# Routing with a scan on VectorE and the rank summed on TensorE, scatters and experts two steps earlier, in a bidirectional Mamba layer with a top-1 mixture of experts

## The chip, the cores and the metric

One core of one Trainium2 chip runs the whole program. The metric is the device time of one execution in microseconds (us). The five engines are TensorE (PE, with its weight loads PEld), VectorE (DVE), ScalarE (ACT), GpSimd (POOL) and SyncE (SP), which here issues nearly all plain DMAs. Each engine works through its own list of instructions in order and waits on semaphores.

## The reference

The input is x, 8 batches of 512 tokens with 128 features, all in float32. It is normalized once to xn, and the output is `x + attn(xn) + ffn(xn)`.

```
xn  = layernorm(x)
attn: xn2 = layernorm(xn)*g + b
      out_f = mamba(xn2), out_b = mamba(xn2 reversed in time), reversed back
      attn  = concat(out_f, out_b) @ combine_w.T + combine_b + xn
mamba: projection, causal convolution of 4 taps, silu, x_proj, softplus(dt), then per step t
      h = h * exp(delta_t * A) + (delta_t * u_t) * B_t ;  y_t = sum_n h[:, n] * C_t[n]
      y = (y + u * D) * silu(z) ;  y @ out_w.T
ffn:  e(token) = argmax over 8 experts of xn @ router_w.T      (the first of equals)
      ffn = down_w[e] @ ( silu(gate_w[e] @ xn) * (up_w[e] @ xn) )
```

The inner width of the Mamba is 256 and its state has 16 entries per channel. There are 4096 tokens in all.

## The kernel before

**The Mamba part sets the pace.** There are 16 units: each of the 8 batches forward and backward (`UNITS`). A unit is cut into `NSTEP` = 16 steps m, so the main loop of every engine runs over m = 0 to 255 and a few more. In a step, the engines do this for 128 rows x 2 states x 512 times: ScalarE computes the decays dA (L1002), TensorE spreads delta*u over the partitions (`spread_du`, L600), VectorE multiplies by B (`du_B`, L1195) and runs the recurrence with `tensor_tensor_scan` (`scan`, L1212 forward, L1214 backward), GpSimd multiplies the states by C (L1435), and TensorE sums over the states (`sum_states`, L634). `du_B` is done for two steps at an even m, and `scan` for two steps at the following odd m. The states lie in a ring of `NH` = 13 buffers: scan m waits for the sum that frees the buffer of m - 13. Sums are taken for groups of 8 steps: the sum of the group from 8g on is placed at TensorE's steps 8g+12 and 8g+13, and its first half needs GpSimd's multiplication of step 8g+6, its second half that of step 8g+7. So the 61st scan (m = 61) needs GpSimd's multiplication of step 54. Projections of the next unit, its softplus and its DMAs are placed at fixed distances from the unit's first step (`fronts`, `front_step`).

**Routing.** From `R0` = 27 on, function `route` is called for two parts per step, each ahead of one `du_B` or `scan`. It finds the expert of each of 4096 tokens (32 columns of 128 partitions), makes the one-hot `one` (128 x 8 experts x 32 columns), and from it the position of each token in the list sorted by expert, in which each expert begins at a multiple of 128. For that TensorE multiplies the one-hot by a strictly triangular matrix (tokens on lower partitions) and by ones (all tokens of a column) at step R0+3 = 30 (L840, L841), and VectorE scans the column sums over the columns. The results are `pos_u` (L1311) and `ej_i` (L1316), the expert of each of 39 tiles of 128 sorted tokens. Nearly each part waits for the part before it by the semaphore `dve_route`; since a `du_B` or `scan` stands between them, the wait is then over.

**Scatters.** GpSimd writes the tokens with 32 indirect DMAs to their positions in DRAM (L1446), from step R0+6 = 33 on, 4 in 2.5 steps, each behind GpSimd's multiplication by C of that step. SP loads the normalized tokens for them (L470), eight loads from step R0+5 on, with two buffers.

**Experts.** From `F0` = R0+29 = 56 on, one tile of 128 sorted tokens starts every 3.5 steps: SP loads the tile and the weights of its expert (a register is loaded from `ej_i`), TensorE multiplies (L784, L807, L802), ScalarE applies silu, GpSimd multiplies gate by up. The last tile ends at step 207.

**Gathers.** From `G0` = 206 on, for each batch b, GpSimd gathers the tokens' results with 4 indirect DMAs, 2 steps behind `gather_step(b)` (L1408, L1411); for six of the batches TensorE adds them to the attention output 7 steps behind `gather_step(b)` (`final_mm`, L702 and L704), ScalarE copies the sum and SP stores it. The gathers stand at steps 208, 212, 216, 220, 224, 228, 232 and 236.

The order on each engine is thus written out by these step numbers; inside a step it is that of the code in the engine's loop.

## Time and profile before

| | us |
|---|---|
| runs: median of 3 (all three) | 912.49 (912.49, 917.79, 912.06) |
| the profiled execution | 918.05 |
| its span | 916.1 |
| VectorE busy | 882.0 (96%) |
| GpSimd busy | 801.0 (87%) |
| TensorE busy | 743.8 (81%) |
| ScalarE busy | 696.9 (76%) |
| granted TensorE clock, mean | 0.886 of full speed |

The span is the time from the first to the last instruction of the profiled execution; 1.95 us of its time lie outside. VectorE is busy nearly all the time, so its few idle stretches and its own work add up to the span. The timeline view gives for each row the start, the duration, the engine and line, and in brackets how long the engine stood idle before it and what released it. VectorE's records overlap: an instruction that needs nothing from the one before it starts before that one's record ends, so what an instruction costs is read from its start to the next start.

### The profile page before, as it was taken

The numbers are of one execution on the slowest core, as the hardware profiler recorded it, in microseconds if no ns is written. First come the engines' busy times: TensorE is split into PE (matmuls) and PEld (weight loads), VectorE is DVE, ScalarE is ACT, GpSimd is POOL, SyncE is SP. The second block draws the span as 40 slices with busy tenths as digits, with TensorE's granted clock in tenths as the row PEclk, the third lists the DMA queues.
The fourth block names the chain that finished last, engine by engine and source line by source line (L and its number), as shares of the span: only waits on it lengthen the run. The fifth ranks groups of instructions, "written<-read, shape, count | busy, mean of one in ns | idle before, by whom it ended". The sixth has DMA issues, their size and how long they took to land. (4 is left out here: it accounts for less than half of the span.)

```text
span 916.1 us, 10763 instructions
## 1 busy us (share of the span) xinstructions
PE 743.8 (81%) x3045; PEld 331.8 (36%) x3045; DVE 882.0 (96%) x633; ACT 696.9 (76%) x1185; POOL 801.0 (87%) x450
## 2 busy tenths in 40 slices
PE   8889866877489978889798987989979879788376
PEld 4434321331034534354443533435333432223022
DVE  5999999999899999999899999999999999999987
ACT  4898965746379889888889889997979976575540
POOL 1578787999999999898898988999798999999995
PEclk9969889787799989989799998989999897979689
DMA  7795443235355555645455636555553534553300
GB/s 216 200 287 122 129 103 103 87 101 136 92 140 178 134 188 146 189 106 127 156 130 178 158 78 195 139 167 148 174 141 99 141 87 153 118 173 73 91 0 12
DMA packets 87371, 123.52 MB, mean 135 GB/s; under 512 B 7945, under 2 KB 58634, under 8 KB 83346
## 3 DMA queue, kind: packets, MB, share of 16 engines
q1 hardware_dynamic: 85266, 118.65, 46.9%
q0 software_dynamic: 2048, 4.20, 1.5%
q8 instruction: 25, 0.41, 0.2%
q14 instruction: 32, 0.26, 0.1%
HBM read 75.50 MB, written 14.29 MB: 98 GB/s over the span
## 5 line engine op out<-in xcount | busy, mean ns | idle before, releaser
L1435 POOL TENSOR_TENSOR hs<-hs,C_rep 128x1024 f32<-128x1024 f32 x250 | 585.7, 2362 | 46.7 <-DVE hs L1214 26.1
L1002 ACT ACTIVATE dA<-delta_rep,A_sb 128x511 f32<-128x511 f32 x512 | 335.4, 717 | 22.8 <-DMA delta_rep<-tmpA 18.6
L1195 DVE TENSOR_TENSOR in_b<-in_b,B_rep 128x1024 f32<-128x1024 f32 x256 | 300.2, 1217 | 12.2 <-PE in_b L600 10.5
L1214 DVE TENSOR_TENSOR_SCAN hs<-dA,in_b 128x1024 f32<-128x1024 f32 x128 | 285.5, 2269 | 5.1 <-PE y L634 5.1
L1212 DVE TENSOR_TENSOR_SCAN hs<-dA,in_b 128x1024 f32<-128x1024 f32 x128 | 285.3, 2269 | 1.0 <-PE y L634 1.0
L600 PE MATMUL in_b<-du,cst 128*128 128x512 f32 x256 | 159.1, 707 | 68.5 <-DVE hs L1214 49.6
L634 PE MATMUL y<-hs,cst 128*32 128x512 f32 x1016 | 136.3, 655 | 22.3 <-POOL hs L1435 22.3
L561 PE MATMUL front<-xpad,w_in 128*128 128x512 f32 x248 | 117.6, 609 | 8.5 <-ACT xi L931 6.4
L1011 ACT ACT_TABLE_LOAD x71 | 91.1, 1283 | 11.6 <-PE moe L784 7.1
L600 PEld LDWEIGHTS in_b<-du,cst 128*128 128x128 f32 x256 | 47.5, 216 | 142.7 <-issue 139.8
L561 PEld LDWEIGHTS front<-xpad,w_in 128*128 128x128 f32 x248 | 46.1, 195 | 64.0 <-issue 48.7
L634 PEld LDWEIGHTS y<-hs,cst 128*32 128x32 f32 x1016 | 28.3, 116 | 105.1 <-issue 67.2
L575 PE MATMUL front<-xpad,w_in 128*128 128x512 f32 x62 | 45.6, 828 | 17.1 <-ACT tmpB L967 11.5
L1376 POOL TENSOR_TENSOR tmpA<-tmpA,tmpB 128x512 f32<-128x512 f32 x31 | 39.5, 1273 | 13.7 <-ACT tmpB L977 13.7
L593 PE MATMUL front<-tmpB,w_dt 8*128 8x512 f32 x62 | 41.3, 750 | 9.2 <-ACT tmpB L953 7.1
L625 PE MATMUL y<-xi,diag_D 128*128 128x512 f32 x62 | 42.4, 772 | 7.8 <-ACT yg L985 6.5
L784 PEld LDWEIGHTS moe<-xsT,gu_w 128*128 128x128 f32 x234 | 33.0, 203 | 36.1 <-issue 36.1
L784 PE MATMUL moe<-xsT,gu_w 128*128 128x128 f32 x234 | 36.1, 294 | 9.7 <-ACT ys L1071 7.2
L1418 POOL TENSOR_TENSOR yg<-yg,zs 128x512 f32<-128x512 f32 x28 | 35.6, 1270 | 9.5 <-ACT yg L985 9.4
L802 PEld LDWEIGHTS moe<-dn_w,th_f 128*128 128x128 f32 x234 | 33.2, 202 | 26.3 <-issue 19.2
L584 PE MATMUL front<-xi,w_x 128*40 128x512 f32 x64 | 35.5, 683 | 7.9 <-ACT xi L944 7.9
L1381 POOL TENSOR_TENSOR du<-tmpA,xi 128x512 f32<-128x512 f32 x31 | 39.5, 1273 | 2.4
(158 smaller groups left out, 813.7 us busy)
## 6 DMA issues: line engine op xcount, KB each, us to landing
delta_rep<-tmpA SPq DMA_DIRECT2D x126, 256.0 KB, 3.9
C_rep<-dbc_scratch SPq DMA_DIRECT2D x16, 1024.0 KB, 7.1
B_rep<-dbc_scratch SPq DMA_DIRECT2D x15, 1024.0 KB, 5.1
gu_w<-in_gate_up SPq DMA_DIRECT2D x39, 384.0 KB, 3.7
dn_w<-in_down SPq DMA_DIRECT2D x39, 192.0 KB, 2.6
xs<-sorted_tokens SPq DMA_DIRECT2D x39, 64.0 KB, 3.8
sorted_ffn<-ys SPq DMA_DIRECT2D x39, 64.0 KB, 2.5
sorted_tokens<-up_f SPq DMA_DIRECT2D x9, 256.0 KB, 4.6
```

Source lines behind the costliest of these rows:

```text
L561: i = e.matmul((M if v == 0 and h else F)[:, :], w_in[:, d, k, h * P:(h + 1) * P], xpad[:, at:at + L], start=(k == 0), stop=(k == NTAP - 1))
L575: e.matmul((M if v == 0 and h else F)[:, :], w_in[:, d, NTAP, h * P:(h + 1) * P], xpad[:, 3:3 + L], start=True, stop=True).then_inc(pe_z, 1)
L600: e.matmul(in_b[:, 2 + 2 * (j % 2), :], spread(j), du[:, du_slot(v, j // 4), :], start=True, stop=True).then_inc(pe_du, 1)
L625: e.matmul(Y[:, :], diag_D[:, 2 * (u % 2) + h, :], xi[:, u % 2, h, :], start=True, stop=False, skip_group_check=True).then_inc(pe_skip, 1)
L634: i = e.matmul(Y[c * DD:(c + 1) * DD, :], sel, hs[:, (m + 2 * c + rh) % NH, r * L:(r + 1) * L], start=False, stop=(rh == 1 and r == RH - 1 ...
L784: i = e.matmul(M[:, c * P:(c + 1) * P], gu_w[:, w, 0, c * P:(c + 1) * P], xsT[:, n % 2, :], start=True, stop=True)
L1002: i = e.activation(dA[:, m % NA, r * L + 1:(r + 1) * L], src, ACT.Exp, scale=A_sb[:, d, 2 * p + jj, RH * rh + r:RH * rh + r + 1])
L1011: e.preload_act_table_set(name)
L1195: e.tensor_tensor(to, in_b[:, 2 + 2 * odd, :].unsqueeze(1).broadcast_to([P, RH, L]), by, ALU.mult).then_inc(dve_mult, 1)
L1212: e.tensor_tensor_scan(to, a[:, 0:n], b, 0.0, ALU.mult, ALU.add).then_inc(dve_scan, 1)
L1214: e.tensor_tensor_scan(to[:, ::-1], a[:, 1:n + 1][:, ::-1], b[:, ::-1], 0.0, ALU.mult, ALU.add).then_inc(dve_scan, 1)
L1435: e.tensor_tensor(hs[:, m % NH, :], hs[:, m % NH, :], C_rep[:, u % 2, RH * rh:RH * rh + RH, :].rearrange("p r t -> p (r t)"), ALU.mult).th ...
```

## The change

Four things are changed.

- **The rank.** VectorE scans the one-hot over the columns (a new `tensor_tensor_scan`, part 3), result `upto`, before TensorE's part; TensorE then adds both parts of the rank in one PSUM group: ones times `upto`, plus (triangle minus 1) times `one`, and the totals of the experts from 8 columns of `upto`. The copy, the subtraction and the addition of 256 columns on VectorE (L1272, L1277, L1286) go; the old scan (L1275) goes, too.
- **The tiles' experts** are computed with the tile's number on the partition: one comparison and one sum over 8 columns in place of 312 columns (L1305, L1312). SP reads a tile's expert from partition n.
- **Fewer parts.** Route has parts 0 to 11 in place of 0 to 17; in five places two instructions of one part follow each other with a wait of the second for the first and nothing between. TensorE's part is at step 29 in place of 30.
- **Two steps earlier.** The loads for the scatters and the scatters start at R0+3 and R0+4 in place of R0+5 and R0+6, F0 is R0+27 = 54 in place of 56, and with it G0 is 204 in place of 206. `FOUR` is bound to LAST and stays 244.

```diff
-F0 = R0 + 29
+F0 = R0 + 27
 G0 = F0 + 7 * NTILE // 2 + 14
-FOUR = gather_step(GATHER_ORDER[-1]) + 10
+FOUR = LAST - 12
...
-        N_ONE, N_POS, N_TILE_EXPERT = 5, 19, 21
+        N_ONE, N_POS, N_TILE_EXPERT = 6, 16, 18
...
-                    if R0 + 5 + 20 * c // 8 == m:
+                    if R0 + 3 + 20 * c // 8 == m:
...
-                    ex = e.value_load(ej_i[0:1, n:n + 1], min_val=0, max_val=E - 1)
+                    ex = e.value_load(ej_i[n:n + 1, 0:1], min_val=0, max_val=E - 1)
...
-                if m == R0 + 3:
+                if m == R0 + 2:
                     e.wait_ge(dve_route, N_ONE)
-                    e.matmul(M[:, 0:256], tri, scratch(0), start=True, stop=True)
-                    e.matmul(M[:, 256:512], ones[:, :], scratch(0), start=True, stop=True).then_inc(pe_route, 1)
+                    upto = scratch(1)
+                    e.matmul(M[:, 256:256 + E], ones[:, :], upto[:, NBLK - 1::NBLK], start=True, stop=True)
+                    e.matmul(M[:, 0:256], ones[:, :], upto, start=True, stop=False)
+                    e.matmul(M[:, 0:256], tri, scratch(0), start=False, stop=True).then_inc(pe_route, 1)
...
+                elif part == 3:
+                    e.wait_ge(dve_route, 5)
+                    e.tensor_tensor_scan(upto, notfirst, one, 0.0, ALU.mult, ALU.add).then_inc(dve_route, 1)
+                elif part == 6:
+                    e.wait_ge(pe_route, 1)
...
                 elif part == 7:
-                    e.wait_ge(pe_route, 1)
-                    e.tensor_copy(val, M[:, 256:512]).then_inc(dve_route, 1)
-                elif part == 8:
-                    e.wait_ge(dve_route, 6)
-                    e.tensor_tensor_scan(cum, cst[:, C_NOTFIRST:C_NOTFIRST + 256], cum, 0.0,
-                                         ALU.mult, ALU.add).then_inc(dve_route, 1)
-                    e.tensor_tensor(pref, M[:, 0:256], val, ALU.subtract).then_inc(dve_route, 1)
...
-                    e.tensor_tensor(
-                        te.rearrange("p (n e) -> p n e", e=E), end_p.unsqueeze(1).broadcast_to([P, NTILE, E]),
-                        cst[:, C_TILE:C_TILE + NTILE].unsqueeze(2).broadcast_to([P, NTILE, E]),
-                        ALU.is_le).then_inc(dve_route, 1)
+                    e.tensor_scalar(te, end_p, cst[:, C_TILE:C_TILE + 1], None, ALU.is_le).then_inc(dve_route, 1)
...
-                        if R0 + 6 + (20 * c + 5 * k) // 8 == m:
+                        if R0 + 4 + (20 * c + 5 * k) // 8 == m:
```

The first scatters on GpSimd. Before, from its multiplication of step 30 on (`hs<-hs,C_rep` is that multiplication, `sorted_tokens` the scatter):

```order
L1435 TENSOR_TENSOR hs<-hs,C_rep 128x1024 [waits dve_scan] x2
L1435 TENSOR_TENSOR hs<-hs,C_rep 128x1024 [waits in_bc0,dve_scan]
L1435 TENSOR_TENSOR hs<-hs,C_rep 128x1024 [waits dve_scan]
L1446 DMA sorted_tokens<-attn_in,pos_u 4992x128 [waits out_clear,dve_route,in_sort0]
L1446 DMA sorted_tokens<-attn_in,pos_u 4992x128
L1435 TENSOR_TENSOR hs<-hs,C_rep 128x1024 [waits dve_scan]
L1446 DMA sorted_tokens<-attn_in,pos_u 4992x128 x2
```

With the change:

```order
L1423 TENSOR_TENSOR hs<-hs,C_rep 128x1024 [waits dve_scan] x2
L1434 DMA sorted_tokens<-attn_in,pos_u 4992x128 [waits out_clear,dve_route,in_sort0]
L1434 DMA sorted_tokens<-attn_in,pos_u 4992x128
L1423 TENSOR_TENSOR hs<-hs,C_rep 128x1024 [waits in_bc0,dve_scan]
L1434 DMA sorted_tokens<-attn_in,pos_u 4992x128 x2
L1423 TENSOR_TENSOR hs<-hs,C_rep 128x1024 [waits dve_scan]
```

Two scatters now stand ahead of the multiplications of steps 32 and 33.

VectorE where the routing ends. Before, the last parts around the `du_B` and `scan` of steps 34 and 35:

```order
L1301 TENSOR_TENSOR gu_w<-moe,gu_w 128x256 [waits dve_route]
L1195 TENSOR_TENSOR in_b<-in_b,B_rep 128x1024 [waits dve_scan,pe_du]
L1304 TENSOR_REDUCE small<-gu_w 128x32 [waits dve_route]
L1305 TENSOR_TENSOR th_f<-moe,cst 128x312
L1195 TENSOR_TENSOR in_b<-in_b,B_rep 128x1024 [waits dve_scan,pe_du]
L1311 CAST pos_u<-small 128x32 [waits dve_route]
L1312 TENSOR_REDUCE gu_w<-th_f 128x39
L1212 SCALAR_TENSOR_TENSOR hs<-dA,in_b 128x1024 [waits dve_mult,act_decay,pe_y]
L1316 TENSOR_SCALAR ej_i<-gu_w 128x39 [waits dve_route]
```

With the change the same stands around the two scans of step 31 and the first `du_B` of step 32:

```order
L1289 SCALAR_TENSOR_TENSOR moe<-small,moe 128x256 [waits dve_route]
L1293 TENSOR_TENSOR gu_w<-moe,gu_w 128x256 [waits dve_route]
L1215 SCALAR_TENSOR_TENSOR hs<-dA,in_b 128x1024 [waits dve_mult,act_decay,pe_y]
L1296 TENSOR_REDUCE small<-gu_w 128x32 [waits dve_route]
L1297 TENSOR_SCALAR gu_w<-moe,cst 128x8
L1215 SCALAR_TENSOR_TENSOR hs<-dA,in_b 128x1024 [waits dve_mult,act_decay,pe_y]
L1300 CAST pos_u<-small 128x32 [waits dve_route]
L1301 TENSOR_REDUCE gu_w<-gu_w 128x1
L1196 TENSOR_TENSOR in_b<-in_b,B_rep 128x1024 [waits dve_scan,in_bc0,pe_du]
L1304 TENSOR_SCALAR ej_i<-gu_w 128x1 [waits dve_route]
```

The positions `pos_u` are written three steps sooner, and L1289 to L1293 is one of the pairs with a wait and nothing between.

TensorE at step 235 and around it, where `final_mm` (L702, L704) of batch 5 stands. Before it came at step 237, behind the sums; with the change:

```order
L678 MATMUL front<-comb_bias,ones 128x512 [waits act_z]
L600 MATMUL in_b<-du,cst 128x512 [waits dve_scan,pool_du]
L702 MATMUL moe<-attn_in,cst 128x512 [waits in_attn1,act_fin]
L704 MATMUL moe<-gu_w,cst 128x512 [waits in_gather1]
L685 MATMUL front<-x_in,cst 128x512 [waits act_base]
L710 MATMUL front<-w_out,yg 128x128 [waits pool_gated]
L710 MATMUL front<-w_out,yg 128x128 x3
L710 MATMUL front<-w_out,yg 128x128 [waits pool_gated]
L710 MATMUL front<-w_out,yg 128x128 x3
L634 MATMUL y<-hs,cst 32x512 [waits dve_C,pool_C]
```

The wait for the gathered rows now stands ahead of the residual, the output projection and the sum.

## Rows read from the trace of the kernel before

**Rows 1.** The page: busy time of each engine, and the chain that ended last.

```profile
PE 743.8 (81%) x3045; PEld 331.8 (36%) x3045; DVE 882.0 (96%) x633; ACT 696.9 (76%) x1185; POOL 801.0 (87%) x450
...
POOL 15%; issue 9%; PE 5%; ACT 4%; DVE 1%; ACTq 0%; POOLq 0%
```

**Rows 2.** Waits of VectorE: us in total, times, longest.

```profile
DVE in_b L1195 <- PE in_b L600: 10.5, 7, 3.7
DVE hs L1214 <- PE y L634: 5.1, 2, 2.8
```

**Rows 3.** Timeline of VectorE, routing: start, us, engine, line, operation [idle before].

```profile
131.05 0.41 DVE L1272 COPY gu_w<-moe 128x256 f32<-128x256 f32 x1
131.38 1.22 DVE L1195 TENSOR_TENSOR in_b<-in_b,B_rep 128x1024 f32<-128x1024 f32 x1
...
141.10 0.16 DVE L1292 TENSOR_TENSOR moe<-small,moe 128x8 f32<-128x8 f32 x1
141.17 0.16 DVE L1293 COPY moe<-small 128x8 f32<-128x8 f32 x1
...
147.91 0.47 DVE L1305 TENSOR_TENSOR th_f<-moe,cst 128x312 f32<-128x312 f32 x1
148.30 1.22 DVE L1195 TENSOR_TENSOR in_b<-in_b,B_rep 128x1024 f32<-128x1024 f32 x1
149.43 0.17 DVE L1311 CAST pos_u<-small 128x32 uint32<-128x32 f32 x1
149.51 0.47 DVE L1312 TENSOR_REDUCE gu_w<-th_f 128x39 f32<-128x312 f32 x1
149.90 2.28 DVE L1212 TENSOR_TENSOR_SCAN hs<-dA,in_b 128x1024 f32<-128x1024 f32 x1
```

**Rows 4.** Timeline of VectorE at the start.

```profile
23.25 0.69 DVE L1343 TENSOR_TENSOR tmpA<-tmpA,tmpB 128x512 f32<-128x512 f32 x1 [1.18 <-ACT tmpB L977]
23.97 0.69 DVE L1346 TENSOR_TENSOR du<-tmpA,xi 128x512 f32<-128x512 f32 x1
24.59 0.68 DVE L1348 COPY w_out<-y 128x512 f32<-128x512 f32 x1
```

**Rows 5.** Timeline of GpSimd ahead of the first scatter: steps 32 and 33, and it.

```profile
143.60 2.34 POOL L1435 TENSOR_TENSOR hs<-hs,C_rep 128x1024 f32<-128x1024 f32 x1 [2.96 <-DVE hs L1212]
146.11 2.37 POOL L1435 TENSOR_TENSOR hs<-hs,C_rep 128x1024 f32<-128x1024 f32 x1 [0.17 <-DVE hs L1212]
150.46 1.19 POOL L1446 DMA_INDIRECT sorted_tokens<-attn_in,pos_u  x1 [1.99 <-issue]
```

**Rows 6.** Timelines behind the last scatter: GpSimd's steps 53 to 55.

```profile
238.99 6.95 POOL L1435 TENSOR_TENSOR hs<-hs,C_rep 128x1024 f32<-128x1024 f32 x3
```

**Rows 7.** The same stretch on TensorE and VectorE.

```profile
243.68 3.38 PE L634 MATMUL y<-hs,cst 128*32 128x512 f32 x16 [10.30 <-POOL hs L1435]
...
247.13 2.29 DVE L1214 TENSOR_TENSOR_SCAN hs<-dA,in_b 128x1024 f32<-128x1024 f32 x1 [2.80 <-PE y L634]
```

**Rows 8.** Timelines near the end: first gather, TensorE's wait for GpSimd, VectorE's waits.

```profile
742.54 1.01 POOL L1408 DMA_INDIRECT gu_w<-sorted_ffn,pos_u  x1 [0.16 <-issue]
...
844.63 4.46 DVE L1212 TENSOR_TENSOR_SCAN hs<-dA,in_b 128x1024 f32<-128x1024 f32 x2 [0.89 <-PE y L634]
...
865.33 3.64 PE L634 MATMUL y<-hs,cst 128*32 128x512 f32 x16 [7.43 <-POOL hs L1435]
...
869.04 2.29 DVE L1214 TENSOR_TENSOR_SCAN hs<-dA,in_b 128x1024 f32<-128x1024 f32 x1 [2.27 <-PE y L634]
...
875.02 2.36 DVE L1195 TENSOR_TENSOR in_b<-in_b,B_rep 128x1024 f32<-128x1024 f32 x2 [3.69 <-PE in_b L600]
```

**Rows 9.** Gather of batch 4 (its last DMA), its addition on TensorE, median landing.

```profile
821.37 0.95 POOL L1408 DMA_INDIRECT gu_w<-sorted_ffn,pos_u  x1 [0.30 <-issue]
...
824.83 1.02 PE L704 MATMUL moe<-gu_w,cst 128*128 128x512 f32 x2
...
gu_w<-sorted_ffn,pos_u POOLq DMA_INDIRECT x24, 2.6
```

More of the change, by code:

```diff
@@ L207, in mamba_moe_kernel @@
         pos_u = sb("pos_u", [P, NBLK], U32)
-        ej_i = sb("ej_i", [P, NTILE], I32)
+        ej_i = sb("ej_i", [P, 1], I32)
         small = sb("small", [P, 64])
@@ L1242, in route @@
             def route(part):
-                one, val, pref, tmp = (scratch(i) for i in range(4))
-                rank, cum = M[:, 0:256], M[:, 256:512]
-                ntile, end_p, first, end = M[:, 0:E], M[:, E:2 * E], M[:, 2 * E:3 * E], small[:, 0:E]
-                te = th_f[:, :, :].rearrange("p a c -> p (a c)")[:, 0:NTILE * E]
+                one, upto, pos, tmp = (scratch(i) for i in range(4))
+                rank, notfirst = M[:, 0:256], M[:, 256:512]
+                total, ntile = M[:, 256:256 + E], M[:, 256 + E:256 + 2 * E]
+                first, end_p = small[:, E:2 * E], M[:, 256 + 2 * E:256 + 3 * E]
                 ke, ek = "p (k e) -> p k e", "p (e k) -> p e k"
-                best, low = small[:, 0:32], small[:, 32:64]
+                best, low, end, te = small[:, 0:32], small[:, 32:64], small[:, 0:E], tmp[:, E:2 * E]
                 if part == 0:
@@ L1279, in route @@
                     e.wait_ge(dve_route, 8)
-                    total = cum.rearrange(ek, e=E)[:, :, NBLK - 1:NBLK].broadcast_to([P, E, NBLK])
-                    thr = cst[:, C_THR:C_THR + NBLK].unsqueeze(1).broadcast_to([P, E, NBLK])
-                    e.tensor_tensor(tmp.rearrange(ek, e=E), total, thr, ALU.is_gt).then_inc(dve_route, 1)
-                elif part == 10:
+                    e.tensor_tensor_scan(end, ones[:, 0:E], ntile, 0.0, ALU.mult, ALU.add).then_inc(dve_route, 1)
                     e.wait_ge(dve_route, 9)
-                    e.tensor_reduce(ntile, tmp.rearrange(ek, e=E), AX_X, ALU.add).then_inc(dve_route, 1)
-                    e.tensor_tensor(pref, pref, cum, ALU.add).then_inc(dve_route, 1)
-                elif part == 11:
-                    e.wait_ge(dve_route, 11)
-                    e.tensor_tensor_scan(end, ones[:, 0:E], ntile, 0.0, ALU.mult, ALU.add).then_inc(dve_route, 1)
-                elif part == 12:
-                    e.wait_ge(dve_route, 12)
@@ new lines, in route @@
+                        rank.rearrange(ek, e=E), first.unsqueeze(2).broadcast_to([P, E, NBLK]), float(P),
+                        rank.rearrange(ek, e=E), ALU.mult, ALU.add).then_inc(dve_route, 1)
+                    e.wait_ge(dve_route, 12)
+                    e.tensor_tensor(pos, rank, one, ALU.mult).then_inc(dve_route, 1)
+                elif part == 9:
+                    e.wait_ge(dve_route, 13)
+                    e.tensor_reduce(low, pos.rearrange("p (e k) -> p k e", e=E), AX_X, ALU.add).then_inc(dve_route, 1)
+                    e.tensor_scalar(te, end_p, cst[:, C_TILE:C_TILE + 1], None, ALU.is_le).then_inc(dve_route, 1)
+                elif part == 10:
+                    e.wait_ge(dve_route, 15)
+                    e.tensor_copy(pos_u[:, :], low).then_inc(dve_route, 1)
+                    e.tensor_reduce(tmp[:, 0:1], te, AX_X, ALU.add).then_inc(dve_route, 1)
+                elif part == 11:
+                    e.wait_ge(dve_route, 17)
+                    e.tensor_scalar(ej_i[:, :], tmp[:, 0:1], float(E - 1), None, ALU.min).then_inc(dve_route, 1)
@@ L1463, in shape_constants @@
     c[:, C_ID:C_ID + P] = np.eye(P)
-    c[:, C_TRI:C_TRI + P] = np.triu(np.ones((P, P)), 1)
+    c[:, C_TRI:C_TRI + P] = np.triu(np.ones((P, P)), 1) - 1.0
     c[:, C_SEL:C_SEL + DD] = np.repeat(np.eye(DD), G, axis=0)
```

43 lines of the change are left out of this document (16 added, 27 removed).

## The prediction

> **What bounds the kernel now.** I read the page first: VectorE is busy for 882.0 of 916.1 us and GpSimd for 801.0, while the chain that ended last spends more on GpSimd (15%) than on any other engine [rows 1]. So the pace is VectorE's, and what a change can win is VectorE's own work or one of its idle stretches. Then the waits of VectorE: 10.5 us in seven waits for TensorE's spread of delta*u, and 5.1 us in two waits for a sum over the states, the longest 2.8 us [rows 2]. The timelines then say where these are. One is at 247 us, right behind the scatters: TensorE had waited 10.30 us for GpSimd before that sum [rows 7]. The others that belong to GpSimd are near the end, behind the gathers: 0.89, 2.27 and 3.69 us, together 6.85 us, and TensorE had waited 7.43 us for GpSimd there [rows 8]. What remains of the waits for the spread, 10.5 - 3.69 = 6.8 us in six, lies between: four of them, about 5.4 us, while experts run.
>
> **VectorE's own work.** Costs go from start to next start. A 256-column instruction costs 131.38 - 131.05 = 0.33 us, the 312-column ones 148.30 - 147.91 = 0.39 and 149.90 - 149.51 = 0.39 us, an 8-column one 0.07 us [rows 3]. Removed: copy, subtraction and addition, 3 x 0.33 = 0.99, and the two 312-column ones, 0.78: 1.77 us. The scan is the same size before and after (nothing). Added: two 8-column instructions, 2 x 0.07 = 0.14. The new waits: five times an instruction needs the one just ahead of it. What that costs is seen at the start: with such a need the next start is 23.97 - 23.25 = 0.72 us on, without it 24.59 - 23.97 = 0.62, for equal instructions [rows 4], so 0.10 each, 0.50 in all. Bounds: nothing, and 0.2 each (twice what the row shows), which gives 1.0. Net on VectorE: 1.77 - 0.14 - 0.50 = **1.1 us less**, between 0.6 and 1.6.
>
> By the Trainium skill (VectorE: DVE Perf Modes, section "The DRAIN you can't avoid") a semaphore after each instruction of a chain costs nothing extra, and one should minimize the count of instructions. By that rule the net would be 1.6 us; the rows above differ from it by 0.10 us per pair, and I go by them.
>
> Before, the old kernel had done nine routing instructions when the scan of step 31 ended; the new one has done all but the last three. At about 0.33 us each, with 0.43 for the one-hot's strided write, 0.59 for the scan and 0.52 for the last reduction, that is 3.3 us before and 4.9 us now. So VectorE reaches the end of step 31 some 1.6 us later than before, and is ahead only from step 33 on.
>
> TensorE's three matmuls instead of two, at step 29: they stand behind the same sum as before, since TensorE has nothing at step 30 ahead of them, and VectorE's part 6 asks for them after two scans (4.4 us). Cost nothing; if that cover were gone, an 8-column and one more 256-column matmul, under 1 us.
>
> **GpSimd and the stall at 247 us.** From the first scatter (150.46) to step 55's multiplication GpSimd works without a gap worth naming, and this stretch ends in the multiplications of steps 53 to 55, 238.99 to 245.94 [rows 6]. TensorE's sum starts with the end of step 54's (243.6) and takes 3.4 us, and VectorE's 61st scan waits 2.80 us for it [rows 7]. Ahead of the stretch GpSimd idles 2.96 + 0.17 + 1.99 = 5.1 us: twice for VectorE's scan, and then for `pos_u`, which is written at 149.43 [rows 3, 5]. With the change `pos_u` is written at about 140 us and two scatters stand ahead of step 32's multiplication, so these idle times are filled by scatters. The stretch begins after step 31's multiplication, which is 1.6 us later. All work up to step 54 is the same 32 scatters and the same multiplications, so it ends 5.1 - 1.6 = **3.5 us** earlier. VectorE without its wait would be at this scan at 247.13 - 2.80 - 1.1 = 243.2; the sum is there at 247.13 - 3.5 = 243.6. So a wait of 0.4 us stays, and the gain at this point is 3.5 us, of which 1.1 is the saved work (now hidden in the end of the GpSimd stretch) and 2.4 the wait. Between, scatters come two steps earlier among the multiplications, 3.2 scatters of 1.3 us more ahead of each; step 46's is then 0.8 us later than before and the 53rd scan finds its sum just in time. If it doesn't, VectorE loses lead that it hasn't got to use, since GpSimd's stretch decides at 247.
>
> SP: its waits for scatters come two steps sooner too. The loads for chunks 5 and 7 now stand ahead of two pairs of delta loads and hold them about 4 us; ScalarE has those decays some 10 us ahead of VectorE. Cost nothing. The first expert tile is loaded two steps earlier, when the scatters end 8 us earlier. Nothing.
>
> **The experts, steps 54 to 205.** Same instructions, shifted by two steps against the projections of the units. A tile takes 3.5 steps and a unit 16, so a shift by two puts at unit v what four tiles later stood at unit v+1: the same meetings, except that forward and backward units change roles. I take the 5.4 us of waits there as unchanged, with 0 and 11 (twice) as bounds.
>
> **The gathers and the end.** GpSimd is behind from the first gather at 742.54 on, until TensorE's wait ends at 865.33 [rows 8]. Moving eight gathers two steps ahead changes their order among the multiplications but not the sum of work up to step 238's, and GpSimd had stood idle under 1 us in the two steps ahead. So the end of that stretch stays where it is against VectorE: gain 0 to 0.7 us, I take 0. What is late next: `final_mm`. Before, the last DMA of gather 4 was issued at 821.37, lands 2.6 us later, and TensorE takes it at 824.83, just in time [rows 9]. Now the gather comes only one gather's place earlier (about 2 us), and TensorE asks 7 us earlier: it waits some 5 to 6 us, and again for batch 5, with the spread for VectorE queued behind. VectorE then loses some 2.5 to 5 us near 830 to 848 us. It has 6.85 us of waits ahead of 875.02 that this fills, so it costs nothing.
>
> **Sum.** Against the profiled execution: span 916.1 - 3.5 = 912.6, its time 918.05 - 3.5 = 914.6. The profiled execution lies 5.6 us above the median of the runs, 912.49, of which one was at 917.79; against the median the forecast is **909.0 us**.
>
> **Rivals.**
>
> 1. *Only VectorE's work counts*, since GpSimd's stretch doesn't end earlier (the scatters wait for their loads, or the sum at step 52 holds TensorE): 912.49 - 1.1 = 911.4. For it: the margins at steps 46 and 52 are under 1 us. Against: the 5.1 us of idle time are plain.
> 2. *The end shrinks too.* If the two steps let GpSimd clear its backlog before step 238, the 6.85 us go as well: 912.49 - 3.5 - 6.85 = 902.1. Against: GpSimd has no idle time there to fill.
> 3. *Slower: the experts meet the projections worse.* The spread (L600) is queued behind a tile's matmuls while TensorE waits for ScalarE. Before this cost VectorE 5.4 us; if it doubles, and the gain is only rival 1's, the time is 912.49 - 1.1 + 5.4 = 916.8, and with the full gain 914.4. It decides from a sum of such waits above 5.4 + 3.5 = 8.9 us on.
> 4. *The late `final_mm`.* TensorE's two waits of 6.0 and 4.7 us all reach VectorE and exceed the 6.85 us by 3.8: 912.49 - 3.5 + 3.8 = 912.8, no change. It decides where TensorE runs at half clock between the two, so that its matmul pairs take 2 us in place of 1.
> 5. *The change doesn't do what it says:* the waits between pairs on VectorE cost far more than 0.2 us. Ten times the row's 0.10 would be 5 us on VectorE; it would hit the start of the scatters as well. 912.49 + 3 = 915.5.
>
> **Chances.** Forecast 0.45, rival 1 0.14, rival 2 0.08, rival 3 0.18, rival 4 0.10, rival 5 0.05. About 1% (9 us) is what a measurement of this kernel can tell from no change. Nearly all cases lie within it; only rival 2 with fewer meetings on TensorE reaches below 903.4, and only rival 3 with worse ones goes above 921.6. Faster by over 1%: 0.08; within 1%: 0.87; slower: 0.05. The range takes the forecast with its bounds, most of rival 3, and the spread of the runs of one kernel (5.7 us between lowest and highest of three): 904.5 to 915.5.
>
> **What would show it.** Right: `pos_u` written near 140 us and the first scatter near 142; no idle time of GpSimd at steps 32 and 33; VectorE's wait at the 61st scan under 1 us and that scan starting near 243.6; routing on VectorE 5.1 us in place of 6.2; near the end, `final_mm` of batches 4 and 5 with waits of TensorE for a DMA, new waits of VectorE between 825 and 850 us, and a smaller wait before the scan at step 245, whose sum still follows GpSimd's step 238. Wrong: a wait at the 53rd scan that carries through, a first scatter later than 145 us, VectorE's waits for L600 in the experts' stretch far from 5.4 us, or a stretch of GpSimd behind the gathers that ends elsewhere against VectorE's step 206.

## The result and the profile after

| | before | after |
|---|---|---|
| median of six runs, us | 913.3 (912.06 to 917.79) | 942.75 (937.41 to 946.78) |
| profiled execution, us (span) | 918.05 (916.1) | 942.36 (940.3) |
| VectorE busy / idle in the span, us | 882.0 / 34.1 | 898.9 / 41.4 |

The changed kernel takes 1.0304 times as long, with a 95% interval of 1.0272 to 1.0336: 29 us **slower**. Forecast were 909.0 us, within a range of 904.5 to 915.5 us; the time lies far above it.

The page answers to [rows 1]: busy time of each engine, and the chain that ended last. Lines are one further on in this kernel (L1196 is `du_B`, L1213 and L1215 the scans, L1222 VectorE's own product with C), and GpSimd's product with C is L1423.

```profile
PE 743.4 (79%) x3047; PEld 331.2 (35%) x3047; DVE 898.9 (96%) x630; ACT 697.6 (74%) x1185; POOL 802.0 (85%) x450
...
issue 26%; PE 8%; DVE 4%; ACT 3%; POOL 0%; ACTq 0%; DVEq 0%
```

VectorE is busy for 16.9 us more, though it has three instructions fewer. GpSimd, which had held 15% of the chain, has none of it. Waits of VectorE, in answer to [rows 2]:

```profile
DVE in_b L1196 <- PE in_b L600: 15.7, 13, 3.1
...
DVE hs L1213 <- PE y L634: 3.9, 3, 1.9
DVE hs L1213 <- ACT dA L1004: 3.3, 3, 1.6
DVE hs L1215 <- PE y L634: 2.7, 1, 2.7
```

That is 13 waits for the spread of delta*u in place of 7, and 7.3 us of idle time more in all. The busy time is the first surprise, and one row holds most of it. VectorE's and GpSimd's timelines at step 56, the first with a scan ahead (start, us, engine, line, operation, [idle before]):

```profile
227.44 4.46 DVE L1215 TENSOR_TENSOR_SCAN hs<-dA,in_b 128x1024 f32<-128x1024 f32 x2
231.81 13.31 DVE L1222 TENSOR_TENSOR hs<-hs,C_rep 128x1024 f32<-128x1024 f32 x1
245.04 2.35 DVE L1196 TENSOR_TENSOR in_b<-in_b,B_rep 128x1024 f32<-128x1024 f32 x2
```

```profile
231.25 11.55 POOL L1423 TENSOR_TENSOR hs<-hs,C_rep 128x1024 f32<-128x1024 f32 x5
242.77 1.25 POOL L1364 TENSOR_TENSOR tmpA<-tmpA,tmpB 128x512 f32<-128x512 f32 x1
244.11 2.13 POOL L1369 TENSOR_TENSOR du<-tmpA,xi 128x512 f32<-128x512 f32 x1
```

`C_ON_DVE` = (41, 56, 180, 217, 226, 255) gives six of the 256 products with C to VectorE. Each reads two inputs from SBUF, as GpSimd's products do. Usually one takes 1.2 us; this one takes 13.31. It ends 1.1 us after GpSimd's first gap (0.09 us between L1364, which ends at 244.02, and L1369), and the GpSimd instruction then takes 2.13 us where that line's usual one takes 1.27. At step 217 the same happens:

```profile
793.96 8.02 DVE L1222 TENSOR_TENSOR hs<-hs,C_rep 128x1024 f32<-128x1024 f32 x1
```

```profile
792.68 6.96 POOL L1423 TENSOR_TENSOR hs<-hs,C_rep 128x1024 f32<-128x1024 f32 x3
799.62 1.27 POOL L1364 TENSOR_TENSOR tmpA<-tmpA,tmpB 128x512 f32<-128x512 f32 x1
800.97 2.14 POOL L1369 TENSOR_TENSOR du<-tmpA,xi 128x512 f32<-128x512 f32 x1
```

The six products take 26.4 us together, in the kernel before 9.2: the difference, 17.2, covers the 16.9 us of VectorE's extra busy time.

**The way through the program.** The end of VectorE's scan of step m, read from its timeline, minus the same of the kernel before, in us:

| step | 56 | 74 | 110 | 158 | 206 | 230 | 255 |
|---|---|---|---|---|---|---|---|
| after | -0.2 | +9.6 | +15.8 | +21.0 | +21.0 | +28.0 | +24.2 |

So there are three losses: one between 56 and 62 (at 62 it is +9.0), a second in the experts' stretch up to 158, a third at 217; some 4 us come back at the end.

Such differences are between one execution and one other. The execution of the kernel before is 4.75 us above the median of its runs, and at step 31, where no kernel here has anything new but the routing, the ones with the new routing lie between +0.5 and +3.1. So a difference of 2 or 3 us in one of them says little.

### The profile page after: what moved, and what is told of

Same layout as the page of the kernel before. It is cut to its first block and busy times, and to the rows that moved or that the text cites. A ratio compares the mean times of both kernels' runs of the same rounds, so it can differ in the third digit from the quotient of the medians.

```text
span 940.3 us, 10764 instructions
## 1 busy us (share of the span) xinstructions
PE 743.4 (79%) x3047; PEld 331.2 (35%) x3047; DVE 898.9 (96%) x630; ACT 697.6 (74%) x1185; POOL 802.0 (85%) x450
## 5 line engine op out<-in xcount | busy, mean ns | idle before, releaser
L1423 POOL TENSOR_TENSOR hs<-hs,C_rep 128x1024 f32<-128x1024 f32 x250 | 585.2, 2362 | 60.8 <-DVE hs L1215 40.1
L1196 DVE TENSOR_TENSOR in_b<-in_b,B_rep 128x1024 f32<-128x1024 f32 x256 | 300.3, 1219 | 15.7 <-PE in_b L600 15.7
L1213 DVE TENSOR_TENSOR_SCAN hs<-dA,in_b 128x1024 f32<-128x1024 f32 x128 | 285.7, 2271 | 7.3 <-PE y L634 3.9
L1215 DVE TENSOR_TENSOR_SCAN hs<-dA,in_b 128x1024 f32<-128x1024 f32 x128 | 285.5, 2271 | 2.7 <-PE y L634 2.7
L600 PE MATMUL in_b<-du,cst 128*128 128x512 f32 x256 | 156.1, 695 | 88.2 <-DVE hs L1215 59.8
L634 PE MATMUL y<-hs,cst 128*32 128x512 f32 x1016 | 139.0, 664 | 16.5 <-POOL hs L1423 16.5
L600 PEld LDWEIGHTS in_b<-du,cst 128*128 128x128 f32 x256 | 45.3, 209 | 164.3 <-issue 157.1
L1013 ACT ACT_TABLE_LOAD x71 | 91.1, 1283 | 13.9 <-PE moe L784 10.1
L1364 POOL TENSOR_TENSOR tmpA<-tmpA,tmpB 128x512 f32<-128x512 f32 x31 | 39.5, 1273 | 20.9 <-ACT tmpB L979 20.9
L593 PE MATMUL front<-tmpB,w_dt 8*128 8x512 f32 x62 | 39.1, 713 | 13.2 <-ACT tmpB L955 6.7
L1369 POOL TENSOR_TENSOR du<-tmpA,xi 128x512 f32<-128x512 f32 x31 | 41.2, 1329 | 2.4
L625 PE MATMUL y<-xi,diag_D 128*128 128x512 f32 x62 | 40.3, 736 | 3.2 <-ACT yg L987 2.2
L1434 POOL DMA_INDIRECT sorted_tokens<-attn_in,pos_u x32 | 32.8, 1025 | 8.1 <-issue 6.6
```

The lines of the kernel that those rows point to most:

```text
L600: e.matmul(in_b[:, 2 + 2 * (j % 2), :], spread(j), du[:, du_slot(v, j // 4), :], start=True, stop=True).then_inc(pe_du, 1)
L625: e.matmul(Y[:, :], diag_D[:, 2 * (u % 2) + h, :], xi[:, u % 2, h, :], start=True, stop=False, skip_group_check=True).then_inc(pe_skip, 1)
L634: i = e.matmul(Y[c * DD:(c + 1) * DD, :], sel, hs[:, (m + 2 * c + rh) % NH, r * L:(r + 1) * L], start=False, stop=(rh == 1 and r == RH - 1 ...
L1013: e.preload_act_table_set(name)
L1196: e.tensor_tensor(to, in_b[:, 2 + 2 * odd, :].unsqueeze(1).broadcast_to([P, RH, L]), by, ALU.mult).then_inc(dve_mult, 1)
L1213: e.tensor_tensor_scan(to, a[:, 0:n], b, 0.0, ALU.mult, ALU.add).then_inc(dve_scan, 1)
```

## The experiments

Medians, and ratios to runs of the kernel before on the same chip, with 95% intervals. "Step 206: +5" means that this scan ends 5 us later than in the kernel before.

### Which part costs: the parts apart

**Routing and scatters without the two steps.** Edit of the changed kernel:

```
-F0 = R0 + 27
+F0 = R0 + 29
-                    if R0 + 3 + 20 * c // 8 == m:
+                    if R0 + 5 + 20 * c // 8 == m:
-                        if R0 + 4 + (20 * c + 5 * k) // 8 == m:
+                        if R0 + 6 + (20 * c + 5 * k) // 8 == m:
```

> The new routing alone: loads, scatters and experts at the steps of before (R0+5, R0+6, F0 = R0+29). By the prediction's sum VectorE has 1.1 us less: 912 us, VectorE's six multiplications by C together near the 9.2 us of before, waits for L600 as before. Rival: the waits between pairs cost much more than 0.1 us: above 915 us.

Measured: 911.95 us, 0.9985 (0.996 to 1.001): no difference that the runs can tell. In its trace VectorE is busy for 880.8 us, 1.2 less than before, and step 56 is 1.1 us ahead, as forecast. The new routing is harmless. At step 206, with the tiles where they were, it stands at -4.2; that is the mark to hold the next numbers against.

**Only the experts' tiles put back**, and with them the gathers (`G0` follows `F0`), scatters still two steps early:

```
-F0 = R0 + 27
+F0 = R0 + 29
```

> The changed kernel with the experts and gathers at the steps of before (F0 = R0+29), scatters still two steps earlier. Theory A: step 56's multiplication still meets GpSimd's run behind the scatters (+12 us), step 217's does not (its record back under 3 us); the experts' waits are back at 5.4 us from 16.7: about 913.3 - 3.5 + 12 = 922 us. Theory B (the experts' phase is the cause of nearly all): 912 to 915 us.

Measured: 922.34 us, 1.0115 (1.0098 to 1.0132). So 20.4 us of the loss hang on the two steps of the tiles and the gathers. The product of step 56 still takes 13.32 us, step 62 is 9.5 us late; the product of step 217 is back at 1.23 us.

**Only the tiles two steps early**, loads and scatters back (the last two edits of the first experiment):

> The changed kernel with the loads and scatters back at their old steps, so that of the moves only the experts' is left, beside the new routing. Theory A (the experts' move costs time by itself, 16 to 20 us between the steps 62 and 230): 926 to 938 us, with VectorE's waits at L600 at 12 us or more, and the record of step 56 at 1.2 us. Theory B (only the combination with the early scatters costs time): 911 to 915 us, with 5 to 7 us of waits at L600.

Measured: 941.06 us, 1.0309 (1.0264 to 1.0354): the whole loss, with a product of 1.2 us at step 56. Step 206: +18.1; the product of step 217 takes 8.1 us there. Theory A; the time is 3 us above its bound. TensorE here waits 8.8 us for the first tile's tokens, which the late scatters bring, but the scan of step 62 is not later for it (-1.6).

### The long product on VectorE

**Without the products of steps 56 and 217** (GpSimd does them):

```
-C_ON_DVE = (41, 56, 180, 217, 226, LAST - 1)
+C_ON_DVE = (41, 180, 226, LAST - 1)
```

> The changed kernel with VectorE's multiplications by C of steps 56 and 217 given back to GpSimd (C_ON_DVE = 41, 180, 226, 255). Theory A, the lock: VectorE's multiplication by C reads two tensors of SBUF and cannot start while GpSimd runs instructions that follow each other without a gap; it was blocked for 12.1 us at step 56 and 6.8 us at step 217. Without the two instructions VectorE loses 13.3 + 8.0 us, GpSimd gets 2 x 2.4 us more: 942.75 - 21 = 922 us, up to 3 us more if GpSimd's backlog shows. Theory B, the experts' new phase explains nearly all and the long records are only VectorE waiting for work that is late anyway: 940 to 943 us.

Measured: 940.54 us, 1.0296 (1.0269 to 1.0323): no gain to speak of, and theory B's time, though not its reason, as the next run shows. Step 62 is 10.3 us earlier than in the changed kernel (-1.3 against +9.0), but by step 80 all but 1 us of it is lost to waits: VectorE waits 22.5 us for L600. In the changed kernel VectorE's long instruction covers these; what they are is the next section's matter. And the product of step 226 now meets GpSimd, which takes back the gain of step 217: between the steps 224 and 230 this run goes from +17.6 to +27.3.

```profile
824.78 10.89 DVE L1222 TENSOR_TENSOR hs<-hs,C_rep 128x1024 f32<-128x1024 f32 x1
```

```profile
825.33 9.25 POOL L1423 TENSOR_TENSOR hs<-hs,C_rep 128x1024 f32<-128x1024 f32 x4
834.75 1.79 POOL L1396 DMA_INDIRECT gu_w<-sorted_ffn,pos_u  x1 [0.16 <-issue]
```

**Gaps in GpSimd's row.** All six products stay, but GpSimd waits, ahead of its products of steps 52 to 58 and 214 to 219, until its own last product is done:

```
+                    if m in (52, 53, 54, 55, 57, 58) or m in (214, 215, 216, 218, 219):
+                        e.wait_ge(pool_C, c_on_pool(m) - 1)
```

> The changed kernel, and GpSimd waits for the end of its own multiplication before it starts the next one, at steps 52 to 55, 57, 58 and 214 to 216, 218, 219 only: the same work, with a short gap between instructions. Theory A (VectorE can take the port at any gap): the multiplications of VectorE at steps 56 and 217 take at most one GpSimd instruction longer, so under 3.7 us each in place of 13.3 and 8.0: about 942.75 - 14 = 928 us. Rival A2 (the port stays with GpSimd as long as it has work waiting, gap or not; or a DMA holds VectorE): both records stay as long, 942 us.

Measured: 939.57 us, 1.0297 (1.0274 to 1.032). VectorE's product of step 56, and GpSimd's row beside it:

```profile
232.64 2.87 DVE L1222 TENSOR_TENSOR hs<-hs,C_rep 128x1024 f32<-128x1024 f32 x1
```

```profile
232.06 13.14 POOL L1425 TENSOR_TENSOR hs<-hs,C_rep 128x1024 f32<-128x1024 f32 x5
```

The same five GpSimd products in a row, with gaps too short for the profile to part them, and VectorE gets in behind the first: 2.87 us in place of 13.31 (2.14 in place of 8.02 at step 217). They take 1.6 us longer together (13.14 against 11.55). The mechanism is thereby shown; the time again doesn't move, against the 928 us that I expected. The waits of the experts' stretch take back the first gain (L600: 21.9 us), and the product of step 226, which was left without gaps, takes 7.71 us here and so takes back the second.

**With the tiles put back, the product moved** from step 56 to 50, where GpSimd still has scatters between its products (edit on the run with the tiles back):

```
-C_ON_DVE = (41, 56, 180, 217, 226, LAST - 1)
+C_ON_DVE = (41, 50, 180, 217, 226, LAST - 1)
```

> The changed kernel with the experts' tiles back at their old steps, and VectorE's second product with C moved from step 56 to step 50, which is ahead of GpSimd's stretch without gaps. Theory A (VectorE is shut out while GpSimd runs two-input instructions without a gap): the record of 13.32 us becomes 1.2 to 3 us, VectorE ends its scans some 10 to 12 us earlier from step 62 on, and the time falls from 922.3 to 909 to 912 us. Theory B (the late experts, or the scatters, cost those 10 us in another way, and the long record only hides that wait): the time stays between 918 and 923 us, and the waits at L600 grow by about 10 us.

Measured: 911.65 us, 0.9975 (0.9952 to 0.9999). The six products take 7.3 us together, the longest 1.3. One number is worth 10.7 us here, as theory A has it: 922.34 to 911.65.

**The same in the kernel before**, one number changed to make it collide:

```
-C_ON_DVE = (41, 56, 180, 217, 226, LAST - 1)
+C_ON_DVE = (41, 58, 180, 217, 226, LAST - 1)
```

> The kernel before with one number changed: VectorE's product with C at step 58 in place of 56, so that it meets GpSimd's three multiplications and one du multiplication behind one another from 238.99 us on. Theory A: the record grows from 1.2 to about 7 to 8.6 us, less where the rows before left a gap, and the time grows by 3 to 7 us (VectorE had 2.8 us of waits just behind, which the longer record would cover), to 915 to 919 us. Theory B (the long record needs something that only the changed kernel has): the record stays at 1.2 to 2 us and the time at 912 to 914 us.

Measured: 917.94 us, 1.0058 (1.0035 to 1.008). Timelines of VectorE and GpSimd:

```profile
238.67 11.06 DVE L1221 TENSOR_TENSOR hs<-hs,C_rep 128x1024 f32<-128x1024 f32 x1
```

```profile
238.16 9.26 POOL L1435 TENSOR_TENSOR hs<-hs,C_rep 128x1024 f32<-128x1024 f32 x4
247.38 1.26 POOL L1376 TENSOR_TENSOR tmpA<-tmpA,tmpB 128x512 f32<-128x512 f32 x1
248.72 2.13 POOL L1381 TENSOR_TENSOR du<-tmpA,xi 128x512 f32<-128x512 f32 x1
```

The same picture in a kernel without any of the change. The time is theory A's; the record is longer than it said, since I had left out the product that GpSimd took over from step 56 and so expected 8.6 us at most. The loss at step 62 is 6.9 us: 11.06 - 1.2 = 9.9, less the 2.8 us wait of [rows 7] which it covers (7.1).

### The tiles two steps earlier

**Later by seven steps.** Two tiles take seven steps, so F0 = R0 + 34 puts each tile where the changed kernel has one (edit on the run with the moved product):

```
-F0 = R0 + 29
+F0 = R0 + 34
```

> The run with VectorE's product at step 50, whose experts' tiles start 29 steps behind the routing, now with them 34 steps behind it. Two tiles take seven steps, so against the rest of the program every tile stands where it stands in the changed kernel (27 steps), one pair of tiles later. Theory A (place: ScalarE's SiLU of a pair of tiles, with its two table loads, comes just ahead of the z copies that TensorE waits for, as in step 136): the waits at L600 and at the scans come back, 10 us or more between the steps 74 and 160, and the scan of step 206 ends 8 to 15 us later than with 29. Theory B (too early: loads and data of the tiles are not ready two steps earlier): the waits stay at the 10 us or less that they have with 29, and step 206 moves by less than 3 us. The end is in both theories later, since the gathers start five steps later: up to 15 us on the total.

Measured: 932.29 us, 1.0228 (1.0177 to 1.028), 20.6 us more than with 29. Step 206: +9.3, against -2.9 with 29, so 12.2 us are lost by then (the rest comes behind it, where gathers and end are five steps later); the longest wait for L600 between the steps 110 and 158 is 3.09 us, in the changed kernel 3.12. So for most of the stretch the tiles are not too early, they are in the wrong **place** against the units' projections. The start is another matter. The run without the products of steps 56 and 217 goes from -1.3 at step 62 to +7.4 at step 74 and on to +18.9 at 206: 8.7 and 11.5 us. This run goes from -3.2 to -2.9 and on to +9.3: 0.3 and 12.2 us. The place explains the second part; the first, some 8 us, belongs to where the first tiles start.

**28 and 30 steps:**

> The same kernel with the tiles 28 steps behind the routing. Theory A (place): a value of its own, anywhere from 909 to 930 us, since other blocks' z copies meet the SiLU steps. Theory B (too early): half way, some 917 to 922 us.

> The same kernel with the tiles 30 steps behind the routing. Theory A (place): a value of its own, 909 to 925 us. Theory B (too early): no worse than with 29, 909 to 913 us.

Measured: 926.85 us, 1.0181 (1.0132 to 1.023), and 929.58 us, 1.0195 (1.0153 to 1.0237). The first is theory A; the second is above what either theory said (925 at most). A later start is no better than an earlier one: of five starts tried (34 has the places of 27), 29 is the only good one.

**What is in the wrong place: ScalarE's SiLU.** For a pair of tiles ScalarE loads the SiLU table and the other one again. ScalarE at steps 135 to 138 of the changed kernel:

```profile
514.37 1.28 ACT L1013 ACT_TABLE_LOAD   x1
515.66 0.49 ACT L1089 ACTIVATE th_f<-moe 128x384 f32<-128x384 f32 x1
...
516.79 1.28 ACT L1013 ACT_TABLE_LOAD   x1
518.08 1.33 ACT L1004 ACTIVATE dA<-delta_rep,A_sb 128x511 f32<-128x511 f32 x2
519.32 0.56 ACT L939 COPY zs<-front 128x512 f32<-128x512 f32 x1
...
523.08 0.58 ACT L939 COPY zs<-front 128x512 f32<-128x512 f32 x1
```

and TensorE, which can't go on before each z copy is done:

```profile
519.94 1.13 PE L575 MATMUL front<-xpad,w_in 128*128 128x512 f32 x2 [1.95 <-ACT zs L939]
523.71 2.07 PE L678 MATMUL front<-comb_bias,ones 1*128 1x512 f32 x2 [2.65 <-ACT zs L939]
525.71 2.07 PE L600 MATMUL in_b<-du,cst 128*128 128x512 f32 x2
```

and VectorE behind that spread:

```profile
527.82 2.37 DVE L1196 TENSOR_TENSOR in_b<-in_b,B_rep 128x1024 f32<-128x1024 f32 x2 [2.52 <-PE in_b L600]
```

The granted clock over steps 135 to 140 is 0.85 here, where TensorE keeps pausing, and 1.00 in the run with the moved product: the pairs of the last two rows of TensorE take 2.07 us (the level of 1.2 GHz), there 1.12. As an estimate, 2 x 2.07 - 2 x 1.12 = 1.9 of VectorE's 2.52 us are due to the lower clock, which came down while TensorE paused for the copies; no run parts the two. With the tiles 29 steps behind, ScalarE has both z copies (the later one is the first row) ahead of the table load:

```profile
502.72 0.57 ACT L939 COPY zs<-front 128x512 f32<-128x512 f32 x1
503.31 1.28 ACT L1013 ACT_TABLE_LOAD   x1
```

```profile
503.34 1.12 PE L678 MATMUL front<-comb_bias,ones 1*128 1x512 f32 x2 [1.14 <-ACT zs L939]
504.40 1.12 PE L600 MATMUL in_b<-du,cst 128*128 128x512 f32 x2
```

The Trainium skill (ScalarE: Activation LUTs, section "What ACT_TABLE_LOAD costs") gives about 1283 ns for a table load, and that is each row's length here.

**Without the tiles' SiLU.** On the run without the products of steps 56 and 217, the experts' gate is copied instead (this kernel doesn't compute the experts' SiLU):

```
-                        table(SILU_SET)
-                        e.activation(th_f[:, n % 3, :], M[:, 0:IFP], ACT.Silu).then_inc(act_gate, 1)
+                        e.activation(th_f[:, n % 3, :], M[:, 0:IFP], ACT.Identity).then_inc(act_gate, 1)
...
-                        e.activation(t, t, ACT.Silu).then_inc(act_thf, 2)
+                        e.activation(t, t, ACT.Identity).then_inc(act_thf, 2)
```

> The run without the product at step 56 (940.5 us), with the tiles 27 steps behind the routing, and the SiLU of the experts' gate replaced by a plain copy of the same size; so the two table loads of a pair of tiles fall away, some 2.56 us of ScalarE's time for each of 19 pairs (this kernel doesn't compute the experts' SiLU). Theory A (place): TensorE's waits for the z copies around step 136 and VectorE's waits behind them go, VectorE's waits at L600 fall from 22.5 us to under 12 us, and the scan of step 206, 18.9 us later than before the change, ends less than 8 us later. Theory B (TensorE's own matmuls and weight loads are what is in the way): the waits fall by less than 4 us, and the time stays at 936 us or more.

Measured: 930.99 us, 1.0207 (1.0165 to 1.0248); ScalarE's table loads fall from 71 to 35 and its busy time from 697.2 to 650.1 us. Step 206: +8.2 in place of +18.9. That is theory A just outside of what it said (under 8 us), and VectorE's waits for L600 fell only to 16.9 us, not under 12. The edit takes the table loads away instead of moving them; that it is their place that counts, and not their number, rests on the run with 29 steps, which has all 71 and stands at -2.9. TensorE's waits around the experts' weights tell what is left:

```profile
  DMA gu_w<-in_gate_up: 24.1, 6
```

**The loads.** SyncE issues gu_w, the weights of a tile's expert, in this kernel behind the two 1 MB loads of a unit's B and C:

```profile
280.30 0.54 SPq L397 DMA_DIRECT2D B_rep<-dbc_scratch  x1
280.88 0.59 SPq L397 DMA_DIRECT2D C_rep<-dbc_scratch  x1
282.25 0.36 SPq L483 DMA_DIRECT2D gu_w<-in_gate_up  x1
```

```profile
290.58 1.62 PE L784 MATMUL moe<-xsT,gu_w 128*128 128x128 f32 x6 [5.52 <-DMA gu_w<-in_gate_up]
```

It arrives about 8 us later, where the median of all gu_w loads is 3.6. In the run with 29 steps SyncE has the same three as gu_w (276.66), B_rep (277.19), C_rep (277.78). TensorE's wait for gu_w in all: 2.5 us in the kernel before, 2.8 with 29 steps and the moved product, 17.5 without the products of steps 56 and 217. The first experts' tile has its own case: SyncE holds its load behind a pair of delta loads that waits for GpSimd. In the run without the products of steps 56 and 217:

```profile
247.94 1.20 SPq L408 DMA_DIRECT2D delta_rep<-tmpA  x2
251.39 0.36 SPq L483 DMA_DIRECT2D gu_w<-in_gate_up  x1
```

**Only the first two tiles' loads earlier** (on the run without the products of steps 56 and 217, from which the last two rows are):

```
-                for n in tiles_at(m, 5):
+                for n in [n for n in tiles_at(m, 5) if n >= NW] + [n for n in tiles_at(m, 0) if n < NW]:
```

> The run without the product at step 56, and with the gu_w loads of the first two experts' tiles issued five steps earlier, ahead of the pair of delta loads that waits for GpSimd. Theory A (SyncE's queue: gu_w stood behind the delta pair, TensorE waited 6.25 us for it and VectorE 3.84 us for TensorE): both waits go or fall under 1.5 us, the scans from step 68 on end 3 to 8 us earlier than without this edit, and the time is 932 to 937 us. Theory B (TensorE has too much to do in the stretch, the load only happens to end last): the waits are put down to other releasers, and the time stays within 1.5 us of 940.5 us.

Measured: 938.5 us, 1.0268 (1.0219 to 1.0316), within what the runs can tell of the 940.54 without the edit. TensorE's wait of 6.25 us for the load goes. Step 74 comes 4.9 us earlier, of which 2.6 us are there at step 31 already, before the edit can act. And TensorE then waits 3.92 us for ScalarE's yg at 252.62 us, VectorE still 2.61 us for TensorE, and at step 158 it is 1.5 us later than without the edit: later places take back what was gained. My forecast of 932 to 937 us was too good.

**All loads one step earlier**, the first two tiles' five steps, with the experts' SiLU and without:

```
-                for n in tiles_at(m, 5):
+                for n in [n for n in tiles_at(m, 4) if n >= NW] + [n for n in tiles_at(m, 0) if n < NW]:
```

> The same two edits of the gu_w loads on the run without the product at step 56 (940.54 us), which keeps the experts' SiLU. Theory A (loads and SiLU add up): the scan of step 206, 18.9 us late, comes 5 to 8 us earlier, the time is 932 to 936 us. Theory B (the SiLU's place alone decides, and covers the loads): step 206 moves by less than 2 us, and the time stays at 939 us or more, as it did with the first two tiles' loads alone.

> The run without the experts' SiLU (930.99 us; this kernel doesn't compute it either), with every gu_w load one step earlier, and those of the first two tiles five steps earlier. In that run TensorE waited 24.1 us in 6 times for gu_w, which stood behind the two 1 MB loads of B_rep and C_rep. Theory A (SiLU's place and the loads' place are the whole cost of tiles two steps earlier): TensorE's waits for gu_w fall under 8 us, and the scan of step 206, 8.2 us late, is less than 3 us late. Theory B (something else is left, TensorE's clock or its own work): step 206 stays 6 us or more late.

Measured: with the SiLU 933.41 us, 1.0231 (1.0192 to 1.027), step 206: +11.2. Without it 916.7 us, 1.0034 (1.0007 to 1.006), step 206: **-5.6**, and TensorE has no wait for gu_w at all. At step 206, with the tiles 27 steps behind the routing:

| step 206 | loads as changed | loads earlier |
|---|---|---|
| with the tiles' SiLU | +18.9 | +11.2 |
| without | +8.2 | -5.6 |

The SiLU is worth 10.7 us alone, the loads' place 7.7 alone, and both together 24.5. Some 1.7 us of the 7.7 and 1.6 of the 24.5 are there at step 31 already, as above. The medians say the same: 940.54 us falls by 9.6 without the SiLU, by 7.1 with the loads earlier, and by 23.8 with both. The -5.6 is the level of the routing alone (-4.2) and of the tiles at 29 steps (-2.9): the experts' stretch is accounted for. With the SiLU, 4.4 of the loads' 7.7 us are won between the steps 62 and 74, at the first tiles. (The 8.7 us that the last of them loses between the steps 224 and 230 are the product of step 226 again, as above.)

**Best of both.** The run with 29 steps and the moved product, with the first two tiles' loads earlier (the diff of that edit above):

> The run with the lock moved away (tiles 29 steps behind the routing, VectorE's product at step 50, 911.65 us), and with the gu_w loads of the first two experts' tiles issued five steps earlier. VectorE's wait of 1.56 us at 261.59 us in that run is put down to TensorE. Theory A (the loads hold TensorE there too): 1 to 2 us less, 909.5 to 911 us, faster than the kernel before. Theory B (TensorE waits there for ScalarE's yg, 4.30 us, whatever the loads do): 911 to 913 us.

Measured: 911.28 us, 0.9991 (0.9971 to 1.0011). The same time as the kernel before; theory B. With 0.9975 (0.9952 to 0.9999) the version without this last edit is a quarter of a per cent faster, half a per cent at best, and its interval just excludes no difference.

## Why the prediction was wrong

**VectorE's own work, -1.1 us: right.** With the routing alone step 56 is 1.1 us ahead and VectorE busy for 1.2 us less. The pairs with a wait inside cost about what the row at the start gave, 0.12 us here where it had 0.10: 132.64 - 132.44 = 0.20 us with it, 132.72 - 132.64 = 0.08 without.

```profile
132.44 0.16 DVE L1283 TENSOR_TENSOR_SCAN small<-ones,moe 128x8 f32<-128x8 f32 x1
132.64 0.16 DVE L1285 TENSOR_TENSOR small<-small,moe 128x8 f32<-128x8 f32 x1
132.72 0.16 DVE L1286 COPY moe<-small 128x8 f32<-128x8 f32 x1
...
139.71 0.17 DVE L1300 CAST pos_u<-small 128x32 uint32<-128x32 f32 x1
```

**GpSimd's stretch, -3.5 us: right in its mechanism, and the seed of the first loss.** `pos_u` is written at 139.71 us (forecast: near 140) and the first scatter starts at 142.41 (near 142). Where early scatters have nothing added to them, with the moved product, step 62 is 2.6 us ahead with 29 steps and 3.1 to 3.6 with 28, 30 and 34. But the last scatter now stands two steps earlier, and so the stretch of bare products behind it, at 238.99 us in [rows 6], begins at 231.25 us, just before VectorE's own product of step 56 (at 231.81 us) instead of some 7 us behind it. This effect had no term in the sum, the first of the two steps that failed: I costed what GpSimd does to its own queue, and took VectorE's instructions as fixed in length. In the changed kernel it is 12 us at step 56 and 6.8 us at step 217.

**The experts, "the same meetings": wrong, the larger of the steps that failed.** Forecast were 5.4 us unchanged, with 11 as the upper bound; rival 3, which named the mechanism (the spread queued behind a tile's matmuls while TensorE waits), had at most 916.8 us. The argument was that a shift by two steps (four tiles against a unit) only exchanges forward and backward units. That exchange, which I named and gave no price, is what matters: the z copies of odd units, and a batch's bias and residual matmuls behind them, stand elsewhere than those of even units and repeat every 32 steps. In the 150 steps there are under five such places, and which of them a SiLU pair meets depends on F0. Moved from 29 to 27, the SiLU pair that stood at step 138 behind the z copy stands at 136 ahead of both, and the gu_w load passes behind B_rep and C_rep. Besides, the first tile's load came behind the delta loads. Measured, with the moved product against without the products of steps 56 and 217: step 206 moves from -2.9 to +18.9, 21.8 us, where the forecast had no change and 5.4 us more as its upper bound.

**The end, 0 us: wrong.** The product of step 217 cost 6.8 us by step 230. Nearly 4 of the 28.0 us at step 230 come back by 255, but most of that is not the change's doing: the routing alone wins 2.8 us there as well (-4.5 at step 245, -7.3 at 255). The last wait of [rows 8], 3.69 us, belongs to that one execution; in the traces of the routing alone and of 29 steps with the moved product it is 0.86 us. So the 6.85 us, on which the prediction leant for this stretch and rival 2, are more like 3.9. `final_mm`, rival 4's mechanism, left no mark: in the changed kernel TensorE waits for no gather in that stretch, probably since VectorE's long product of step 217 had held everything back. Where that product is gone, in the run without the products of steps 56 and 217, TensorE waits 4.7 us for gathers in five times.

**Why the two losses don't add up.** From the changed kernel, putting the tiles back gains 20.4 us and then moving the product 10.7. In the other order the products gain 2.2 us, and the way from there to 911.65 us is 28.9. While VectorE is held for 12 us, TensorE, ScalarE and the loads can run ahead, and the first waits of the experts' stretch vanish behind it: between the steps 62 and 74 the changed kernel loses 0.6 us, without the product of step 56 it is 8.7. And without the product of step 217 that of step 226 is held instead. Each is worth its price only where the other is gone.

**The rule that the prediction left out.** The Trainium skill (SBUF — State Buffer, sections "Who interferes with whom" and "SBUF: two separate sides") says that a VectorE instruction with two SBUF inputs contends with a GpSimd instruction that reads SBUF, and that whichever starts first has the shared port pair for the whole instruction, while the other blocks. By that rule, as an estimate from the rows, a product would take 1.2 + 2.4 = 3.6 us at most. The rows of the kernel before bear out one such instruction (the product of step 41 takes 3.05 us, and so the six 9.2 instead of 7.3); the rows after show more than the rule: the loser is shut out for GpSimd's whole unbroken row.

## What to carry to other kernels

Before moving work in time, look for instructions of VectorE and GpSimd that both read two SBUF operands, and see whether the move brings one into a row of the other without gaps: its record's length there, not its usual one, is its price, and a wait of the engine for itself between the row's instructions lets the other in. When two periodic pieces of work share in-order engines, "the same meetings, shifted" has to be checked against the longest period, with the table loads and big transfers of each placed beside the other's waits. And measure the parts of a combined change apart: here the routing, worth a microsecond at most, came with a two-step shift that cost some thirty.

## What the runs showed of the hardware

- VectorE's product with two SBUF inputs waits through a whole row of GpSimd's: 13.31, 11.06, 10.89 and 8.02 us against 1.2 us alone. What it waits for is the rest of the row: with 34 steps the product of step 217 began at 782.26 us in a row that ended at 784.70, and took 3.53 us. Of all its products in the 17 traces 20 took over 2 us (2.14 to 13.32), and each of them ended 1.09 us, to 0.01, behind the end of the last instruction of GpSimd's row. The gap that ends a row can be as short as 0.09 us, and GpSimd's next instruction then takes 2.13 instead of 1.27 us.
- With the scatters' indirect DMAs between GpSimd's products, VectorE's waits for one of them at most: 1.2 us at step 50, and at step 41 either 1.2 us (changed kernel) or 3.05 us (kernel before).
- A 384 KB load issued 1.4 us behind the second of two 1 MB loads arrives after some 8 us, with a median of 3.6 us for all such loads; VectorE, behind TensorE, waits 3.45 us for it.
